# Expert numbers of eight tiles in one integer, for TensorE's register loads

## What is computed

```python
def _L0_ffn_ref(x, gate_w, Wu, Wv, Wo):        # E=8 experts, R=128, K=2
    logits = jnp.einsum('bnd,de->bne', x, gate_w)
    topv, topi = jax.lax.top_k(logits, K)
    w = jax.nn.softmax(topv, axis=-1)
    u = jnp.einsum('bnd,edr->bner', x, Wu)
    v = jnp.einsum('bnd,edr->bner', x, Wv)
    s = jax.nn.silu(u) * v
    Y = jnp.einsum('bner,erd->bned', s, Wo)
    y_sel = jnp.take_along_axis(Y, topi[..., None], axis=2)
    return jnp.einsum('bnkd,bnk->bnd', y_sel, w)
x = x + xattn(_layernorm(x), ctx, ctx, mask, ...)
x = x + _L0_ffn_ref(_layernorm(x), gate_w, Wu, Wv, Wo)
```

## Time and profile before

| | us |
|---|---|
| three runs | 416.37 (median), 415.38, 417.5 |
| the profiled execution | 418.02 |
| its span, the part that the profile shows | 416.3 |
| TensorE busy in it | 399.8 (96%) |
| VectorE busy | 331.7 (80%) |
| ScalarE busy | 278.2 (67%) |
| GpSimd busy | 210.2 (51%) |

### The profile page before, as it was taken

The page is one execution under the profiler, slowest core; times in us unless marked ns, Lnnn a source line. Parts: engine busy times, 40 slices in busy tenths (PEclk is TensorE's granted clock), DMA queues, the critical chain, the costliest instruction groups (busy, mean ns, idle before and its releaser), DMA issues.

```text
span 416.3 us, 10266 instructions
## 1 busy us (share of the span) xinstructions
PE 399.8 (96%) x3031; PEld 356.7 (86%) x3031; DVE 331.7 (80%) x1108; ACT 278.2 (67%) x596; POOL 210.2 (51%) x227
## 2 busy tenths in 40 slices
PE   8999999999999999999999999999999999999990
PEld 5688899999999999998888888789999989999970
DVE  2578899999999999998887888778887667667660
ACT  1777888888988888888767666566666444444430
POOL 2011125665555565655435545452333467888881
PEclk9999999999999999999999999999999999999997
DMA  8813424776767766443695359779966699996892
GB/s 287 282 65 102 119 89 169 255 258 232 255 223 239 236 232 217 169 173 133 185 321 199 131 203 351 277 256 292 320 219 211 206 253 307 276 237 102 126 138 75
DMA packets 49557, 87.66 MB, mean 211 GB/s; under 512 B 7648, under 2 KB 18400, under 8 KB 49376
## 3 DMA queue, kind: packets, MB, share of 16 engines
q1 hardware_dynamic: 35600, 52.37, 39.1%
q0 software_dynamic: 13904, 34.62, 29.0%
HBM read 44.77 MB, written 48.29 MB: 224 GB/s over the span
## 4 chain that ended last, share of the span: by engine, by line
PE 72%; DVE 14%; ACT 4%; issue 3%; SPq 3%; DMA 2%; POOLq 0%; POOL 0%; DVEq 0%; ACTq 0%
PE psQ L1547 12%; PE psQ L1548 12%; PE psQ L1549 12%; PE psT L1543 11%; PE psO L1547 2%; PE psZ L1547 2%; PE psO L1548 2%; PE psO L1549 2%; PE psZ L1549 2%; PE psZ L1548 2%; DVE st L1158 2%; DVE qT L979 2%; PE psQ L1543 2%; DMA xn<-z_dram 2%; PE psS L1547 2%
## 5 line engine op out<-in xcount | busy, mean ns | idle before, releaser
L979 DVE TENSOR_TENSOR qT<-psT,qT 128x512 fp32r<-128x512 f32 x103 | 69.5, 688 | 28.7 <-ACT qT L782 28.1
L629 POOL DMA_INDIRECT z_dram<-zb x64 | 69.4, 1084 | 39.1 <-DVE zb L1267 22.6
L1547 PE MATMUL psQ<-wuv,qT 128*128 x284 | 86.3, 304 | 0.4 <-DVE qT L979 0.4
L1548 PE MATMUL psQ<-wuv,qT 128*128 x284 | 80.2, 282 | 0.0
L1549 PE MATMUL psQ<-wuv,qT 128*128 x284 | 80.1, 282 | 0.0
L1547 PE MATMUL psQ<-qT,wq 128*128 128x256 f32 x256 | 75.2, 294 | 1.5 <-DVE qT L979 1.4
L1549 PE MATMUL psQ<-qT,wq 128*128 128x256 f32 x256 | 72.4, 283 | 0.0
L1548 PE MATMUL psQ<-qT,wq 128*128 128x256 f32 x256 | 72.3, 283 | 0.0
L782 ACT ACTIVATE qT<-psT 128x512 fp32r<-128x512 f32 x103 | 59.5, 595 | 13.6 <-PE psT L1543 13.6
L1547 PEld LDWEIGHTS psQ<-wuv,qT 128*128 128x128 f32 x284 | 53.7, 189 | 5.2 <-issue 1.0
L850 ACT ACTIVATE gate_work<-psQ 128x128 f32<-128x128 f32 x71 | 19.7, 277 | 54.1 <-PE psQ L1549 54.1
(11 more groups left out here) (305 smaller groups left out, 1065.7 us busy)
## 6 DMA issues: line engine op xcount, KB each, us to landing
wq_flat<-z_dram SPq DMA_DIRECT2D x28, 264.0 KB, 5.5
xin<-in_x_dram SPq DMA_DIRECT2D x11, 512.0 KB, 3.6
z_dram<-spare SPq DMA_DIRECT2D x17, 264.0 KB, 4.0
qpT_flat<-z_dram SPq DMA_DIRECT2D x11, 264.0 KB, 5.1
zT_ctxT<-in_x_dram SPq DMA_DIRECT2D x5, 512.0 KB, 3.5
kpT_flat<-z_dram SPq DMA_DIRECT2D x9, 264.0 KB, 4.1
vp_flat<-z_dram SPq DMA_DIRECT2D x9, 264.0 KB, 4.5
xn<-z_dram SPq DMA_DIRECT2D x8, 264.0 KB, 5.4
```

The lines of the kernel that those rows point to most:

```text
L629: pool.indirect_dma_start(out=z_dram, out_offset=bass.IndirectOffsetOnAxis(ap=z_of(b)[:, t, ROW_COL + k:ROW_COL + k + 1].bitcast(U32), axi ...
L979: nc.vector.tensor_tensor(o, a, b, ALU.subtract).then_inc(s, 1)
L1547: pe.matmul(o, w[LO], a[HI], start=first, stop=False)
L1548: pe.matmul(o, w[HI], a[LO], start=False, stop=False)
```

## The change

`PACKS` divides the tiles into words of eight: one word for tiles 8 to 15, one for 17 to 24, six for 25 to 72. Tiles 0 to 7 and 16 are in no word. After `sched_exp` of a part is written, VectorE folds it: neighbours into pairs (second times 8 plus first), pairs into fours (times 64), fours into eights (times 4096), so that a word holds eight numbers of three bits. That is three operations for each part, at tiles 5, 12 (ahead of `plan_used(1)`) and 22 of its loop. TensorE waits for the pack (`packed`) and loads a word at the first of its tiles; the number of a tile is the word shifted right and masked with 7, in a register. Tiles without a word load as before. `sched_exp` becomes two columns longer, and GpSimd sets these to zero at the start, so `CONSTS` is 21.

```diff
+WORD = 8
+PACKS = ((WORD, 1), (EARLY, 1), (FULL, -(-(TILES - FULL) // WORD)))
+WORDS = sum(n for _, n in PACKS)
-CONSTS = 20
+CONSTS = 21
-        sched_exp = sb("sched_exp", [1, TILES], I32)
+        sched_exp = sb("sched_exp", [1, PACKS[2][0] + WORD * PACKS[2][1]], I32)
+        exp_pair = sb("exp_pair", [1, 4 * WORDS], I32)
+        exp_quad = sb("exp_quad", [1, 2 * WORDS], I32)
+        exp_word = sb("exp_word", [1, WORDS], I32)
...
+            nc.gpsimd.memset(sched_exp[:, TILES:], 0).then_inc(const_ready, 1)
...
+            def pack(g):
+                first, n = PACKS[g]
+                w0 = sum(k for _, k in PACKS[:g])
+                steps = [sched_exp[:, first:first + WORD * n], exp_pair[:, 4 * w0:4 * (w0 + n)],
+                         exp_quad[:, 2 * w0:2 * (w0 + n)], exp_word[:, w0:w0 + n]]
+                dve.wait_ge(sched_ready, 2 * g + 2)
+                for k in range(3):
+                    if k:
+                        dve.wait_ge(packed, 3 * g + k)
+                    src = steps[k].rearrange("p (n two) -> p n two", two=2)
+                    nc.vector.scalar_tensor_tensor(steps[k + 1].rearrange("p (n one) -> p n one", one=1), src[:, :, 1:2], float(8 ** (1 << k)), src[:, :, 0:1],
+                                                   ALU.mult, ALU.add).then_inc(packed, 1)
...
+                if t == 5:
+                    pack(0)
                 if t == 6:
                     Choose(last).all()
...
                 if t == 12:
+                    pack(1)
                     plan_used(1)
...
+                if t == 22:
+                    pack(2)
                 if is_held(t + 1):
                     own_of(t + 1)
...
-                    expert[t] = pe.value_load(sched_exp[0:1, t:t + 1], min_val=0, max_val=E - 1)
+                    g, (first, n) = max((g, p) for g, p in enumerate(PACKS) if g == 0 or t >= p[0])
+                    if not first <= t < first + WORD * n:
+                        expert[t] = pe.value_load(sched_exp[0:1, t:t + 1], min_val=0, max_val=E - 1)
+                    else:
+                        if (t - first) % WORD == 0:
+                            pe.wait_ge(packed, 3 * (g + 1))
+                            w = sum(k for _, k in PACKS[:g]) + (t - first) // WORD
+                            expert["word"] = pe.value_load(exp_word[0:1, w:w + 1], min_val=0, max_val=E ** WORD - 1)
+                        expert[t] = pe.snap((expert["word"] >> (3 * ((t - first) % WORD))) & (E - 1))
```

## The result

The changed kernel takes 417.94 us (median of 17 runs, 417.01 to 420.22); the kernel before takes 416.37 (17 runs, 415.07 to 419.57). The ratio is 1.0038, interval [1.0023, 1.0054]: slower by 1.6 us, not faster by 1.0. The profiled execution of the changed kernel took 417.94 with a span of 416.2, so it is a typical one. The one of before that the prediction was worked out on took 418.02, 1.65 over its median. I therefore took a second profile of the unchanged kernel: 416.34, span 414.6.

The account below looks back on a forecast made before the run. TensorE, busy 96% of the span, was taken as the bound. Gains 0.57 + 0.60 less 0.16 and 0.1, with some 0.1 for single loads, made 1.0 us: 416.37 to 415.4 (chance 0.50), range 413.9 to 417.5.

Parts of the forecast that it names:

- Waits for `packed`: TensorE's new waits before tiles 8, 17 and 25: already met on arrival, so zero.
- Shift and mask: TensorE register operations, 0.11 to 0.23 us a tile where 1.1 are free: nothing on the path, except 0.1 at tile 25.
- The second pack: VectorE at tile 12, no idle time: 0.6 us on the path, absorbed by later landing waits.
- the landings at tiles 18 and 19: TensorE's waits for rows to land, 0.62 and 0.48 us, said to absorb the pack at tile 12.
- The first pack: VectorE at tile 5, behind the gate product: covered by 0.87 us of idle time; 0.6 without that cover.
- the third: VectorE's pack at tile 22: delays the gate product some 0.2 us, absorbed by a landing wait of 0.23.
- The loads, 1.0 us: TensorE, 17 loads for 71: long loads from tile 25 on cost 0.57 + 0.60, less 0.16 still exposed; gain 1.0.
- The rule for the room: TensorE: 1.1 us free from load to turn; a load costs nothing up to 0.75 to 0.8 us, beyond that TensorE waits.
- The end: GpSimd's last stores: 0.6 us of room, and they come earlier with TensorE's tiles, so the gain reaches the end.
- D: Rival: shift and mask slow on the sequencer, deciding from over 1.1 us per tile; 421 us, chance 0.03.
- B: Rival, slower: second pack's 0.6 and third's 0.2 on the path if landings come earlier; 417.3 us, chance 0.13.
- A: Rival, no gain: long loads come with DMA traffic and may be fewer in unprofiled runs; 416.4 us, chance 0.20.

Follow-up runs that it names:

- alu_late: Kernel before with 71 loads and no pack, plus a shift and a mask of each expert number behind the wait: 418.96 us, ratio 1.0071.
- after: The changed kernel itself, against the kernel before: 417.94 us, ratio 1.0038.
- hoist: Changed kernel with shift and mask put into a register ahead of the turn's wait: 416.45 us, ratio 1.0015 to the kernel before.
- load_twice: Kernel before with each expert number's load preceded by another full load: 442.06 us, ratio 1.0619.
- alu_ahead: alu_late with its shift and mask put into a register straight behind the load, ahead of the wait: 417.96 us, ratio 1.0033 to the kernel before.
- packs_only: Changed kernel's packs and memset kept, but TensorE loads every expert number as before: 416.62 us, ratio 1.0012 to the kernel before.
- load_ahead: Kernel before with the load of the next tile's expert number moved ahead of the down product: 417.83 us, ratio 1.0051.

## Why the prediction was wrong

- **17 loads for 71**: right. **Waits for `packed`**: right, none shows.
- **Shift and mask, "nothing on the path"**: this is the step that failed. The size was right: I gave 0.11 to 0.23 us a tile, and it is 0.2. The place was wrong. I set it against the 1.1 us of room beside the down product, where the diff writes the expression. It runs behind the turn's wait for the gate product, where 0.3 us are free in an ordinary tile and nothing where TensorE waits for that product. Two operations there cost 2.8 us in alu_late. Tiles 8 to 16 pay 0.82 (alu_late, and after less hoist), tiles 18 to 22 about 0.55 (three periods), tiles 26 to 70 some 0.7 (118.11 and 118.35 in the two kernels with words and late operations, 117.48, 117.73 and 117.21 in the three with the operations ahead). The last of these is no surer than single profiles are: six without the operations differ by 1.0 there. Of the place I had no row, and bounded the price only.
- **The second pack**: the price was said to be 0.6 and is 0.43 (three steps of 0.17, not 0.20). That it lies on the path was right. That the landings at tiles 18 and 19 absorb it was wrong: they are in the first profile and not in the second profile, nor in after. The first pack is covered and the third costs nothing that shows, as said.
- **The loads, 1.0 us**: too large. Over tiles 26 to 70 six kernels with all loads and no register operations added took 118.33, 118.30, 117.54, 117.86, 117.70 and 117.35 (mean 117.85), the three with five loads 117.47 in the mean. That is 0.4, less than the six differ among themselves. The two profiles of before happen to be the dearest of the six. The rule for the room held in kind (load_twice, alu_ahead) and was too generous in size.
- **The end**: I saw GpSimd's last stores and 0.6 us of room there. The store of after that answers to it (GpSimd's timeline):

```profile
406.77 1.02 POOL L696 DMA_INDIRECT out_dram<-qpT_flat  x1 [0.30 <-issue]
```

There is 0.30 before it and not 0.90: GpSimd's row has used that room up.
- **The sum with these terms**: 0.82 + 0.7 for late operations, 0.43 for the pack, 0.2 for the end, less 0.4 for loads is +1.75; measured is +1.6. Left out are tiles 16 to 26, where 0.55 more for late operations and 0.51 less where the second profile has its load of 995 ns nearly cancel. The 0.7 and the 0.4 come from single profiles, so the agreement is in part luck.
- **The rivals**: D named the right operations and the wrong reason. They are not slow; it set its threshold at 1.1 us a tile from the wrong place, and the real room is nothing where the turn waits for the gate product, and 0.3 us in an ordinary tile. B had the pack's part of the loss, and its point of decision (landings that come earlier) was met; its 417.3 came near 417.94 without the late operations. A was right that loads are worth little. Its reason, traffic of the DMAs, is not shown: in the first profile they move 304 GB/s where the median load is 942 ns and 252 where it is 311, but their busy share is 0.93 there and 1.03 here.

## What to carry to other kernels

Of a register value built by an expression, ask where its operations are made: at its first use they may stand behind a wait (find by the trace which wait ends last), in front of the instruction that everything waits for. Put them into a register of their own where the engine has time, and count what else stands in that time (behind a long load it is not free either). Before a wait or a long transfer in a single profile is spent as cover or as gain, take a second profile of the same kernel.

## What the runs showed of the hardware

- A plain register operation of TensorE's sequencer is listed with 32 to 47 ns and takes about 0.1 us from start to start. Two behind a met wait put 0.2 us between two weight loads (0.09 and 0.29). The grouped form for an address takes 46 ns.
- TensorE's sequencer did not run past a turn that waits: in 63 of 70 tiles of after its next register operation began 0.04 to 0.06 us behind the end of VectorE's gate product, though the low half of the turned rows, for which it also waits, had been ready for 1.58 us (median).
- Two late operations in each of 71 tiles cost 2.8 us; four, made into a group and two plain ones, cost 12.9: a threshold, not a slope.
- A load into a register took from 295 to 1618 ns for the same four bytes, with medians of 305 to 363 in the kernels with 71 loads. Long ones recur every 5 to 6 us for a while (287.34, 293.10, 298.91, 304.55 in alu_ahead). I have no run that shows what makes them long.
- GpSimd's last 33 indirect DMAs (30 stores and three loads, 0.99 to 1.59 us each, 0.3 between them), with 8.1 us from the start of the last to the end of the span, make a row of 65.4 us. It set the end in packs_only, alu_ahead, load_ahead and after, where its first store waited 1.6 to 3.8 us for a landing.
